# Loading and preparing the second attention's projection weights during the expert stage of a two-layer decoder kernel

## What is computed

```python
x = x + L0_attn(layernorm(x))            # rotary factor, causal, 4 key/value heads
x = x + L0_xattn(ctx, layernorm(x))      # window of 4 over 77 context rows
x = x + L0_ffn(layernorm(x))             # 8 experts, top 2, capacity 320 rows per batch
x = x + L1_attn(layernorm(x))            # this stage's projection is what the change touches
x = x + L1_xattn(layernorm(x), ctx)
x = x + L1_ffn(layernorm(x))             # 8 experts
```

```python
qkv = x @ W_qkv + b_qkv                  # 2048 x 256 by 256 x 768
q = q / sqrt(16)
score = q k^T + q . rel_emb_k[clip(k - q, -64, 64) + 64]
ctx = softmax(score) v + softmax(score) . rel_emb_v[...]
```

## Time and profile before

| | |
|---|---|
| median of three runs | 1856.06 us |
| lowest and highest run | 1853.22 and 1858.87 us |
| span of the profiled execution, first to last instruction | 1860.8 us |
| mean granted TensorE clock over the span | 0.929 |
| busy over the span: PE, DVE, ACT, POOL | 86%, 56%, 47%, 31% |
| expert stage with both row chains | about 411 to 998 us |
| projection of the second attention | about 998 to 1065 us |
| second attention | about 1065 to 1693 us |
| tail | about 1693 to 1861 us |

### The profile page before, as it was taken

One profiled execution on the slowest core, in us unless ns is written; L12 is line 12 of the kernel. 1 busy time (PEld: TensorE's weight loads), 2 busy tenths in 40 slices (PEclk: granted clock), 3 DMA queues, 4 the chain that ended last, 5 costly groups with the idle time before them and its releaser, 6 DMA issues. The chain is left out here.

```text
span 1860.8 us, 34549 instructions
## 1 busy us (share of the span) xinstructions
PE 1600.7 (86%) x12872; PEld 1085.8 (58%) x12872; DVE 1042.4 (56%) x2132; ACT 876.0 (47%) x1458; POOL 572.3 (31%) x823
## 2 busy tenths in 40 slices
PE   4668989978669999999985569999999999997888
PEld 2423333336546777777652357777777777776544
DVE  4557777716242111111244687888888878882656
ACT  2105666662232111111123467888888778872331
POOL 2301111112412200000233455555555555543111
PEclk9759999997778999999986889999999999998899
DMA  2461112012102133222112768868778687655101
GB/s 85 115 176 22 23 25 42 1 42 85 53 8 91 57 130 105 88 81 88 45 51 86 220 184 202 208 197 199 203 203 210 192 199 200 191 149 174 46 12 34
DMA packets 208006, 210.33 MB, mean 113 GB/s; under 512 B 19523, under 2 KB 186065, under 8 KB 207713
## 3 DMA queue, kind: packets, MB, share of 16 engines
q1 hardware_dynamic: 202977, 194.49, 38.3%
q0 software_dynamic: 4864, 13.64, 2.2%
HBM read 126.06 MB, written 81.81 MB: 112 GB/s over the span
## 5 line engine op out<-in xcount | busy, mean ns | idle before, releaser
L1197 DVE CUSTOM_DVE_ANT_0 prob<-ps,dev 128x1024 f32<-128x1024 f32 x256 | 311.5, 1217 | 2.1 <-DMA skew_p<-prob 2.0
L1094 ACT ACTIVATE prob<-prob,nmax 128x1024 f32<-128x1024 f32 x256 | 293.3, 1146 | 18.1 <-DVE nmax L1197 17.8
L1026 PE MATMUL ps<-cst,prob 128*128 128x128 f32 x2048 | 278.9, 277 | 1.7 <-issue 1.0
L1930 PE MATMUL ps<-xeT,w 128*128 128x320 f32 x896 | 254.1, 445 | 0.9 <-ACT xeT L1965 0.9
L1026 PEld LDWEIGHTS ps<-cst,prob 128*128 128x128 f32 x2048 | 227.3, 141 | 45.0 <-issue 22.6
L744 ACT ACTIVATE pT<-ps 128x512 f32<-128x512 f32 (+3 forms) x384 | 166.1, 495 | 152.4 <-PE ps L704 150.0
L1211 DVE COPY probT<-ps 128x512 f32<-128x512 f32 x256 | 176.3, 689 | 106.4 <-PE ps L1026 106.4
L781 DVE TENSOR_REDUCE nmax<-ps 128x1 f32<-128x128 f32 (+7 forms) x256 | 185.3, 754 | 81.8 <-PE ps L685 80.6
L1930 PEld LDWEIGHTS ps<-xeT,w 128*128 128x128 f32 x896 | 174.2, 196 | 75.8 <-issue 8.8
L1977 ACT ACTIVATE xT_c<-ps 128x320 f32<-128x320 f32 (+1 forms) x91 | 45.4, 499 | 330.2 <-PE ps L1930 330.2
L1101 ACT ACTIVATE probT<-ps 128x512 f32<-128x512 f32 x256 | 151.2, 591 | 105.2 <-PE ps L1026 105.2
(11 more groups left out here) (310 smaller groups left out, 2222.4 us busy)
## 6 DMA issues: line engine op xcount, KB each, us to landing
dev<-skew_u SPq DMA_DIRECT2D x128, 256.0 KB, 3.8
skew_p<-prob SPq DMA_DIRECT2D x128, 256.0 KB, 3.2
w<-in_L_ffn_w SPq DMA_DIRECT2D x27, 896.0 KB, 6.0
skew_u<-cst SPq DMA_DIRECT2D x64, 256.0 KB, 4.0
wr<-skew_p SPq DMA_DIRECT2D x128, 128.0 KB, 2.9
qs<-qd SPq DMA_DIRECT2D x96, 128.0 KB, 3.8
ks<-kd SPq DMA_DIRECT2D x48, 256.0 KB, 5.8
qd<-parts SPq DMA_DIRECT2D x16, 384.0 KB, 2.5
```

Source lines behind the costliest of these rows:

```text
L1026: last = nc.tensor.transpose(ps[:, ring_bank(job), kb * P:(kb + 1) * P], prob_tile(t, (4 * h + kb) * P, (4 * h + kb + 1) * P), k.c("ident"))
L1094: nc.scalar.activation(prob_tile(t, 0, S), prob_tile(t, 0, S), ACT.Exp, bias=nmax[:, t % 4:t % 4 + 1], scale=-1.0).then_inc(s_exp, 1)
L1197: nc.vector.tensor_tensor_reduce(out=prob_tile(t, 0, S), in0=scores, in1=dev_tile(t), scale=-1.0, scalar=3.0e38, op0=ALU.add, op1=ALU.min, ...
L1930: last = nc.tensor.matmul(ps[:, a + z * wide + h, 0:CAP], w[:, j, c, f * P:(f + 1) * P], xeT[:, c, h * CAP:(h + 1) * CAP], start=(c == 0), ...
```

## The change

Three things are done.

1. A new buffer `pre` (2048 floats on each partition) lives through the whole program. The weights `w1`, the value bias `bv1`, the biases `bc1` and the two end rows `rc1` and `rv1` of the second projection lie in it.
2. Their 21 loads leave `project_heads` and go to the end of SP's program in `experts`, with the weights last, and SP waits there until the weights have landed. The four bias instructions leave DVE's program in `project_heads` and go into that of `experts`, behind `shifted(1)` and ahead of the adds of batch 1. In the projection PE's, ACT's and DVE's first waits fall away.
3. Room is made. Chain 1 uses `toT`, `hidT`, `sc`, `cnt`, `tmp`, `gs` and `aT` of chain 0 instead of its own, `wr`, `side1` and `wrT` of the second attention lie in `pre`, and so do `gc` and `yT` of the tail.

No other instruction is added, removed or moved, and no other wait.

```diff
+        self.pre = self.sb("pre", [P, 2048])
+        self.w1 = self.pre[:, 0:DC * 3 * D].rearrange("p (c n) -> p c n", c=DC)
+        self.bv1 = self.pre[:, 1536:1792]
+        self.bc1 = self.pre[:, 1792:1798]
+        self.rc1 = self.pre[:, 1798:1800]
+        self.rv1 = self.pre[:, 1800:1832].rearrange("p (z d) -> p z d", z=2)
...
@@ project_heads
-        w = k.sb("wqkv" + tag, [P, DC, NW], ctx=ctx)
+        w = k.w1 if rel else k.sb("wqkv" + tag, [P, DC, NW], ctx=ctx)
+        bc, bv = k.bc1, k.bv1
...
             def _(sp):
-                if rel:
-                    load_weights(sp)
...
             def _(pe):
-                if rel:
-                    pe.wait_ge(s_w, 16)
...
             def _(act):
-                if rel:
-                    act.wait_ge(s_be, 1)
...
             def _(dve):
-                if rel:
-                    dve.wait_ge(s_b, 16 * (2 + 2 * HG + 2))
-                    by_head = bv[:, :].rearrange("p (h d) -> p h d", d=HD)
-                    nc.vector.tensor_tensor(by_head, by_head, rv[:, 0, :].unsqueeze(1).to_broadcast([P, H, HD]), ALU.add).then_inc(s_bv, 1)
-                    nc.vector.tensor_scalar(bc[:, 0:2], bc[:, 0:2], HD ** -0.5, None, ALU.mult)
-                    nc.vector.tensor_scalar(bc[:, 4:6], bc[:, 2:4], rc[:, 1:2], None, ALU.add).then_inc(s_zone, 1)
-                    dve.wait_ge(s_zone, 1)
-                    nc.vector.tensor_scalar(bc[:, 2:4], bc[:, 2:4], rc[:, 0:1], None, ALU.add).then_inc(s_be, 1)
@@ attention1
-        side1 = k.sb("side1", [P, HQ, P], ctx=ctx)
+        side1 = k.pre[:, 1024:1536].rearrange("p (h w) -> p h w", h=HQ)
-        wr = k.sb("wr1", [P, 2, HQ, P], ctx=ctx)
+        wr = k.pre[:, 0:1024].rearrange("p (s h w) -> p s h w", s=2, h=HQ)
-        wrT = k.sb("wrT1", [P, HQ, P], ctx=ctx)
+        wrT = k.pre[:, 1536:2048].rearrange("p (h w) -> p h w", h=HQ)
@@ RowChain.__init__
-        self.toT = k.sb("turned0" + tag, [P, DC, GT * P], ctx=ctx)
+        self.toT = before.toT if before else k.sb("turned0" + tag, [P, DC, GT * P], ctx=ctx)
...
@@ experts, SP, behind the loads of the last item
+                sp.dma_start(k.bv1[:, :], k.d["L1_attn_b_qkv"][2 * D:3 * D].rearrange("(a n) -> a n", a=1).to_broadcast([P, D])).then_inc(s_b1, 16)
+                sp.dma_start(k.bc1[:, 0:4], k.d["L1_attn_b_qkv"][0:2 * D].rearrange("(s p) -> p s", p=P),
+                             allow_slow_non_contiguous=True).then_inc(s_b1, 16)
+                for z, row in ((0, 0), (1, NR - 1)):
+                    for h in range(HG):
+                        sp.dma_start(k.rc1[h * HD:(h + 1) * HD, z:z + 1], k.d["L1_attn_rel_emb_k"][row:row + 1, :].rearrange("a d -> d a"),
+                                     allow_slow_non_contiguous=True).then_inc(s_b1, 16)
+                    sp.dma_start(k.rv1[:, z, :], k.d["L1_attn_rel_emb_v"][row:row + 1, :].to_broadcast([P, HD])).then_inc(s_b1, 16)
+                sp.dma_start(k.w1[:, :, :], k.d["L1_attn_W_qkv"].rearrange("(c p) n -> p c n", p=P)).then_inc(s_w1, 16)
+                sp.wait_ge(s_w1, 16)
@@ experts, DVE
                 shifted(0)
                 shifted(1)
+                dve.wait_ge(s_b1, 16 * (2 + 2 * HG + 2))
+                by_head = k.bv1[:, :].rearrange("p (h d) -> p h d", d=HD)
+                nc.vector.tensor_tensor(by_head, by_head, k.rv1[:, 0, :].unsqueeze(1).to_broadcast([P, H, HD]), ALU.add)
+                nc.vector.tensor_scalar(k.bc1[:, 0:2], k.bc1[:, 0:2], HD ** -0.5, None, ALU.mult)
+                nc.vector.tensor_scalar(k.bc1[:, 4:6], k.bc1[:, 2:4], k.rc1[:, 1:2], None, ALU.add).then_inc(s_zone1, 1)
+                dve.wait_ge(s_zone1, 1)
+                nc.vector.tensor_scalar(k.bc1[:, 2:4], k.bc1[:, 2:4], k.rc1[:, 0:1], None, ALU.add).then_inc(s_bias1, 1)
+                dve.wait_ge(s_bias1, 1)
                 for g in (2, 3):
```

More of the change, by code:

```diff
@@ L501, in values @@
                     if rel:
-                        if t == 0:
-                            dve.wait_ge(s_bv, 1)
                         nc.vector.tensor_tensor(vz[:, heads, kb, :], src.rearrange("p (h d) -> p h d", d=HD),
@@ L1351, in __init__ @@
         GT = self.GT
-        self.wo = weights_of.wo if weights_of else k.sb("wo0" + tag, [P, DC, D], ctx=ctx)
-        self.gw = weights_of.gw if weights_of else k.sb("gate" + tag, [E, D], ctx=ctx)
+        self.wo = before.wo if before else k.sb("wo0" + tag, [P, DC, D], ctx=ctx)
+        self.gw = before.gw if before else k.sb("gate" + tag, [E, D], ctx=ctx)
         self.gT = k.sb("gateT" + tag, [P, DC, E], ctx=ctx)
-        self.toT = k.sb("turned0" + tag, [P, DC, GT * P], ctx=ctx)
+        self.toT = before.toT if before else k.sb("turned0" + tag, [P, DC, GT * P], ctx=ctx)
         self.xT = k.sb("xT0" + tag, [P, DC, S], ctx=ctx)
@@ L1361, in __init__ @@
         self.shift = k.sb("shift0" + tag, [P, 2 * KB], ctx=ctx)
-        self.hidT = k.sb("hidT" + tag, [PH, 2, GT * P], ctx=ctx)
+        self.hidT = before.hidT if before else k.sb("hidT" + tag, [PH, 2, GT * P], ctx=ctx)
         self.pt, self.lo, self.fl, self.fl2, self.mx, self.sm, self.m1, self.m2 = (
@@ L1365, in __init__ @@
         self.loi = k.sb("loi" + tag, [P, KB], I32, ctx=ctx)
-        self.sc, self.cnt, self.tmp, self.gs = (k.sb("x0_" + n + tag, [P, KB, SC], ctx=ctx) for n in ("sc", "cnt", "tmp", "gs"))
-        self.aT = k.sb("aT" + tag, [SC, 2, GT, P], ctx=ctx)
+        self.sc, self.cnt, self.tmp, self.gs = (
+            (before.sc, before.cnt, before.tmp, before.gs) if before else
+            (k.sb("x0_" + n + tag, [P, KB, SC], ctx=ctx) for n in ("sc", "cnt", "tmp", "gs")))
+        self.aT = before.aT if before else k.sb("aT" + tag, [SC, 2, GT, P], ctx=ctx)
         self.lg, self.ex, self.cand, self.keep, self.base = (
@@ L1374, in __init__ @@
         self.idx_s = k.sb("idx_s" + tag, [P, 2, KB], U32, ctx=ctx)
-        self.s_wo = weights_of.s_wo if weights_of else k.sem(f"s_c{b}_wo")
-        self.s_gw = weights_of.s_gw if weights_of else k.sem(f"s_c{b}_gw")
+        self.s_wo = before.s_wo if before else k.sem(f"s_c{b}_wo")
+        self.s_gw = before.s_gw if before else k.sem(f"s_c{b}_gw")
         (self.s_job, self.s_prep, self.s_turn, self.s_out, self.s_var, self.s_sd, self.s_ch, self.s_shift, self.s_xs,
@@ L1794, in experts @@
         xs1 = chains[1].xn
+        s_w1, s_b1, s_zone1, s_bias1 = (k.sem("s_m1_" + n) for n in ("w", "b", "zone", "bias"))
         s_up = [k.sem(f"s_m_up{j}") for j in range(2)]
@@ L2197, in tail @@
         g1 = k.sb("g1", [P, 2, NF1], ctx=ctx)
-        gc = k.sb("gc1", [P, 2, NF1], ctx=ctx)
+        gc = k.pre[:, 0:2 * NF1].rearrange("p (s n) -> p s n", s=2)
         sg = k.sb("sg1", [P, 2, NF1], ctx=ctx)
@@ L2201, in tail @@
         hT = k.sb("hT1", [P, 2, FC1, NF1], ctx=ctx)
-        yT = k.sb("yT1", [P, DC, NF1], ctx=ctx)
+        yT = k.pre[:, 2 * NF1:4 * NF1].rearrange("p (c n) -> p c n", c=DC)
         (s_wo, s_bo, s_wx, s_in, s_job, s_turn, s_out, s_bias, s_var, s_sd, s_ch, s_shift, s_xs, s_normA, s_normD, s_score, s_exp,
```

25 lines of the change are left out of this document (5 added, 20 removed).

## The result

| | before | changed |
|---|---|---|
| first comparison, median (20 executions each) | 1856.35 us | 1852.52 us |
| profiled execution, span | 1860.8 us | 1852.3 us |
| mean granted TensorE clock | 0.929 | 0.928 |

The ratio is 0.9974, 95% interval [0.9963, 0.9986]: 4.8 us less, between 2.6 and 6.9. The same kernel was measured twice more beside the experiments: 0.9951 [0.9933, 0.9969] and 0.9968 [0.995, 0.9986]. Weighted by their intervals the three give 0.9967, some 6 us.

A forecast was written before the change was run, and what follows sets the result against it. The ring of four buffers was taken to set the projection's end, with PE only 3.2 us ahead. The terms -6.3 + 0 + 0 + 0 took 1856.06 to 1849.8 us, range 1846.0 to 1855.0.

The forecast's parts named there:

- PE's shift: Second projection: without the wait for weights PE starts at 998.9, and all products move 4.3 us earlier.
- the other seam: Earlier seam with the same barrier: SP and PE start within 0.04 us (411.70 and 411.74), the basis for PE's start.
- The start of the ring: Projection's ring of four buffers: units 0 to 3 start 9.1, 7.0, 5.7 and 5.7 us earlier.
- The term of 6.3: Projection's end moves 6.3 us earlier, the middle between smallest lead 5.7 and mean 6.9; bounds 4.3 to 7.5.
- The landing: From SP's last issue to PE's start in the attention; no term of its own, the tail was said to hang on the last stores.
- The stretch: From ACT's last copy in the experts to PE's start in the attention: 67.75 us should become 61.4; 63.4 means PE's pace.
- The first rival: Projection: PE's products set the pace, so the gain is only their 4.3 us shift, 1851.8 us; chance 0.20.
- What I costed at nothing: Loads and four bias instructions in the experts, shared scratch in the row chains, and new addresses: cost 0 each.
- the 1.5 us that I had allowed for at worst: Experts: moved loads holding up the first gathers of batch 0 by 4.3 us, less DVE's 2.8 idle.
- The other rivals: PE's start was hidden work (0.06), DVE's new instructions delay POOL (0.04), new addresses slow the attention (0.05).
- hidden work: Projection: PE's wait for weights hides something else, so it starts no earlier than 1003.18 at worst; 1854.1 us, chance 0.06.
- The sum: Whole kernel: -6.3 us and three zeros, from 1856.06 to 1849.8 us, 0.34% less; forecast's chance 0.65.

The follow-up runs named there:

- room only: Changed kernel with all 21 loads and the four bias instructions back in the projection; shared scratch, `pre` and new addresses stay; 1.0001 of the kernel before.
- early loads: Changed kernel with the 12 loads for the attention's first heads behind the stores of units 9 to 20, not 13 to 23; 0.9967 of the kernel before.
- biases moved: Changed kernel with the weights' load and its wait back in the projection, only the biases staying in the experts; 0.9992 of the kernel before.
- all three: Changed kernel with six ring buffers, attention loads behind the stores of units 9 to 20, and five unread matmuls; 0.9907 of the kernel before.
- early and six: Changed kernel with six ring buffers and attention loads behind the stores of units 9 to 20, no unread matmuls; 0.993 of the kernel before.
- extra matmuls: Changed kernel with five matmuls that nobody reads, keeping PE busy at the end of the experts; 0.9953 of the kernel before.

## Why the prediction was right or wrong, point by point

- **PE's shift** was forecast at 4.3 and was 3.8 at product 15 (43.0 against 46.8; 4.1 against room only). Its start moved by 4.2 as worked out from the other seam; product 1 lost 0.36 to a clock that rose one product later. I had assumed "product 0 at 1.2 GHz and the rest at 2.4 GHz as before".
- **The start of the ring**: forecast leads 9.1, 7.0, 5.7 and 5.7; measured 9.0, 6.5, 5.2 and 5.2. Most of the difference is the same slow product 1.
- **The term of 6.3** was the step that was mis-sized. It was taken midway between the smallest lead and the mean. The last issue gained 5.1, 5.6 and 5.3 us in the three executions, 1.0 less than forecast: the end follows the smallest lead (5.2) and hardly the mean (6.5). The reason stood among my rows: PE was only 3.2 us ahead, so a buffer with a larger lead meets products that are not ready. Four more of ACT's waits than the first are now ended by PE, 14 by stores.
- **The landing** was missing from the sum. I let the stage's end follow the ring one to one, so its change was forecast at nothing. It scattered between 7.6 and 11.1 us (mean 9.1), against 7.7 and 8.6 in the kernel before and "room only". The 0.9 us between the means is less than the scatter, so that the landing took back a part of the gain is not shown. What ends last there is also not the last store, as I had written, but the last load: in the kernel before the store issued at 1055.72 lands 6.7 us later, and the last of the loads issued at 1056.20 lands 7.5 us after its issue, 1.0 us ahead of PE's start. The rows to see the traffic by were there: PE's wait of 18.16 us that reaches 9 us beyond the last issues, and a DMA share of 0.75 in the middle of the stage, which is 0.65 to 0.69 up to 1040 and 0.95 from 1040 to 1045, where the loads come on top. I never read the window of the last 25 us, which is at 0.96:

```profile
1038.50:1063.00 24.50, 8.74 (x29) 5.10 (x27) 14.17 (x25) 9.47 (x16) 9.11 (x9) 0.79 0.96 273
```

- **The stretch** should have been 61.4; it was 63.5, 65.5 and 62.3, mean 63.8, against 67.8 and 68.6. That is 4.4 us gained. I had written that 63.4 would mean PE sets the pace. The number came, the cause did not: six buffers moved unit 23 by over 2 us with the products unmoved, and early loads shortened the stretch. The first rival gave the better size and the wrong mechanism; what bounds the stage is the ring together with nearly full DMA engines, and PE only behind both. How the two share the missing 1.9 us (6.3 less 4.4) stays open, since that is hardly more than one stretch scatters.
- **What I costed at nothing** cost nothing: the 21 issues, the four instructions (0.9 us in a pause that keeps 1.40), shared scratch, and addresses (room only 1.0001, [0.9982, 1.0019]; 93.9 us and 733 ns in POOL's group, unchanged). POOL's first gather of batch 0 did become later, its wait for the store of item 10 rising from 2.02 to 4.71 us, and the pauses behind it took that in: nothing is left of the 1.5 us that I had allowed for at worst.
- **The other rivals** fell. PE's start was no hidden work (1.30 us behind the seam). DVE's new instructions did not hold up POOL: the gathers beside them kept their 1.02 and 0.97 us. Nor were they stretched themselves, as one row of before had made me fear (L2049, 0.40 us): that instruction took 0.17 us in the changed kernel, again beside a gather. No attention of the changed kernel was longer than before's 627.65.
- **The sum.** Forecast 1849.8, measured 1852.5 in the first comparison and, by the other two ratios, 1847 to 1850 (0.9951 and 0.9968 of 1856.06). All lie in the range. The sign was right, the 6.3 us were about 2 too many in the stage itself, and the scatter of the whole kernel is larger than that error. That the three ratios together give some 6 us is luck: the stretch gained 4.4, and the changed kernel's 38 executions had a mean clock of 0.9305 against 0.9295 in 77 of before, which goes with 1.3 us (last section).

## What to carry to other kernels

When a stage ends with stores and prefetches, read the DMA share of its last stretch before you carry an earlier start through to its end. At 0.95 and more the bytes may hold the end, and spreading them is the experiment that tells: here it took 3.5 us off with six buffers. The share alone does not tell, for it was 0.95 and 0.98 also in the kernels whose end followed PE. Two late starts that feed one another (products and ring) have to be moved together; here they were worth 0.4 and 1.7 us apart and over 5 together. And spread prefetches over the stores as early as their own inputs allow, with enough buffers for stores that land later: six buffers and loads four units earlier took the stretch from 62.3 to 65.5 us down to 57.4 (1.4 of it the clock), and the best combination brought the kernel to 0.991 of its first time, clock and all.

## What the runs showed of the hardware that I had not expected

**How early the clock rises goes with the length of a whole stage.** The expert stage took 585.4 to 586.0 us in ten profiled executions and 579.1 to 579.6 in the other four (room only, biases moved, all three, early and six), with the same instructions on every engine up to 900. The granted clock tells the two apart: from 411 to 420 it was 0.50 to 0.57 in the ten and 0.62 or 0.63 in the four, and from 430 to 435 0.66 to 0.75 against 1.00; first the kernel before, then room only:

```profile
430.00:435.00 5.00, 4.29 (x10) 1.76 (x11) 0.23 (x2) 2.22 (x3) 2.17 (x4) 0.66 0.02 6
```

```profile
430.00:435.00 5.00, 5.00 (x26) 3.10 (x26) 1.49 (x5) 2.37 (x6) 1.84 (x3) 1.00 0.01 3
```

Among executions of one kernel an increase of 0.001 in the mean clock goes with some 1.3 us less. Medians of one kernel differ by up to 2.6 us (before) and 4.5 us (changed) from group to group, and single executions by more than the change is worth. The Trainium skill ("TensorE: Matmul & The Clock Gate", section "Part 1: The HAM clock gate (the "warmup" mystery)") says that the number of matmuls at the lower clock varies from run to run with the gate's phase at the start; the windows above agree that the clock rises at different times in the same program, and here 6 us go with it; that the phase is the reason no run shows. Whether the changed kernel meets the better phase more often (11 of 38 executions at 0.932 or more, 14 of 77 of before) stays open.

**Work that nobody reads can pay, and can miss.** Four matmuls in a pause of 7.9 us and one behind it had the clock up for product 0 in "extra matmuls" (1.95 us) and not in "all three" (3.37 us); seven and one had it up in the one execution seen (1.96 us).

**Full DMA engines move less here than elsewhere in the same kernel.** At a share of 0.93 to 0.99 these stretches moved 252 to 297 GB/s, and with the loads where they were the last one took 7.3 to 10.7 us to land. At the start of the expert stage, where loads of 896.0 KB come in and nothing is stored, the engines moved 389 GB/s at a share of 1.03 (kernel before, window 415 to 425). The Trainium skill ("DMA: Bandwidth & Descriptors", section "Specifications") gives about 358 GB/s as a core's limit for transfers to and from HBM. The 389 GB/s are above it, so it was no limit in this case, and the stretches at the end of the projection lie far below it with engines as full. What makes the rates differ, and what makes the last landing scatter, was not found out.
